# A cross-attention kernel: the Gram product of a group in 9 matmuls instead of 12, with its low diagonal handled through a column of the value product

## The reference, cut to what matters

```python
probs_t = softmax(q @ k_t.T * attn_scale)            # per head, 112 x 371
text_out = probs_t @ v_t
qsem = l2norm(probs_t @ text_ehs)                    # per head, 112 x 512
sem = qsem @ l2norm(ip_ehs).T                        # per head, 112 x 4
fused = q @ k_ip.T * attn_scale + 0.5 * sem
probs_ip = softmax(fused) * spatial_mask
out = (text_out + probs_ip @ v_ip) @ W_out + b_out + hidden_states
```

## Time and profile before

| | |
|---|---|
| median of 3 runs | 386.72 us (385.99 to 387.68) |
| profiled execution, first to last instruction (span) | 384.5 us |
| its own time | not on the page |
| mean granted TensorE clock | 0.998 |
| TensorE busy | 374.8 us, 97% |
| VectorE, ScalarE, GpSimd busy | 225.0, 213.2, 208.1 us |
| HBM traffic | 97 GB/s |

### The profile page before, as it was taken

One profiled execution on the slowest core, in us unless ns is written; L12 is line 12 of the kernel. 1 busy time (PEld: TensorE's weight loads), 2 busy tenths in 40 slices (PEclk: granted clock), 3 DMA queues, 4 the chain that ended last, 5 costly groups with the idle time before them and its releaser, 6 DMA issues.

```text
span 384.5 us, 9489 instructions
## 1 busy us (share of the span) xinstructions
PE 374.8 (97%) x3610; PEld 320.3 (83%) x3610; DVE 225.0 (59%) x498; ACT 213.2 (55%) x498; POOL 208.1 (54%) x229
## 2 busy tenths in 40 slices
PE   8999999998999999999999999999999999999996
PEld 6879898777888888888888888888888888888774
DVE  4998462774457536664556646664556656654454
ACT  6834145575556554646556554646555476458742
POOL 7020470675448652796248642796258443855972
PEclk9999999999999999999999999999999999999999
DMA  8999998276027420571227430581207310001000
GB/s 252 321 241 182 201 213 157 82 162 140 9 72 166 78 72 2 157 147 24 76 73 162 81 87 2 160 147 20 77 2 174 59 43 3 2 2 57 2 3 31
DMA packets 30001, 37.88 MB, mean 99 GB/s; under 512 B 14378, under 2 KB 27163, under 8 KB 29275
## 3 DMA queue, kind: packets, MB, share of 16 engines
q1 hardware_dynamic: 29588, 36.87, 41.3%
q10 hardware_dynamic: 368, 0.41, 0.4%
HBM read 28.36 MB, written 8.81 MB: 97 GB/s over the span
## 4 chain that ended last, share of the span: by engine, by line
PE 84%; DMA 6%; DVE 5%; ACT 2%; issue 1%; SPq 1%; DVEq 0%; ACTq 0%
PE PR L1078 39%; PE Y L1078 27%; PE O L1078 9%; PE P L1078 7%; DMA qst<-ma 3%; DVE mx L950 2%; DMA Vt<-wk 2%; PE PR L1269 1%; DMA qd<-kst 1%; PE PR L1206 1%; DVE kst L904 0%; DVE kst L902 0%; ACT big L796 0%; SPq L507 0%; SPq L427 0%
## 5 line engine op out<-in xcount | busy, mean ns | idle before, releaser
L620 POOL TENSOR_TENSOR pb<-pb 128x448 f32<-128x448 f32 x78 | 89.1, 1143 | 97.2 <-DVE pb L974 91.8
L950 DVE TENSOR_REDUCE mx<-PR 112x1 f32<-112x371 f32 x160 | 82.0, 537 | 75.2 <-PE PR L1078 74.9
L1078 PE MATMUL Y<-er,Gh 128*128 128x448 f32 x240 | 95.2, 397 | 0.7 <-ACT er L800 0.3
L974 DVE TENSOR_TENSOR pb<-big,Y 128x448 f32<-128x448 f32 x120 | 72.7, 620 | 33.6 <-PE Y L1078 33.4
L1078 PE MATMUL Y<-er,Gl 128*128 128x448 f32 x240 | 87.2, 363 | 0.0
L796 ACT ACTIVATE big<-P 128x448 f32<-128x448 f32 x120 | 65.2, 544 | 31.6 <-PE P L1078 31.4
L800 ACT ACTIVATE er<-big 128x448 fp32r<-128x448 f32 x120 | 69.3, 578 | 3.8
L1078 PEld LDWEIGHTS Y<-er,Gh 128*128 128x128 f32 x240 | 45.1, 188 | 11.9 <-DVE pb L974 7.8
L1078 PE MATMUL PR<-kst,qst 96*112 96x371 bf16 x160 | 50.6, 329 | 0.5 <-ACT Vt L788 0.2
L1078 PEld LDWEIGHTS Y<-er,Gl 128*128 128x128 f32 x240 | 45.2, 188 | 2.2
L1078 PE MATMUL P<-qst,kst 99*128 99x112 bf16 x480 | 43.0, 213 | 1.6 <-DMA qst<-ma 1.5
(11 more groups left out here) (201 smaller groups left out, 679.9 us busy)
## 6 DMA issues: line engine op xcount, KB each, us to landing
et<-ctxT SPq DMA_DIRECT2D x7, 752.0 KB, 4.4
kst<-kd SPq DMA_DIRECT2D x7, 720.0 KB, 7.7
kd<-ks SPq DMA_DIRECT2D x16, 288.0 KB, 2.9
qst<-qd SPq DMA_DIRECT2D x48, 70.0 KB, 2.4
kst<-kd SPq DMA_DIRECT2D x7, 480.0 KB, 9.7
kst<-kd SPq DMA_DIRECT2D x9, 240.0 KB, 9.2
qd<-kst SPq DMA_DIRECT2D x4, 336.0 KB, 7.7
vx<-xr SPq DMA_DIRECT2D x8, 140.0 KB, 2.7
```

The lines of the kernel that those rows point to most:

```text
L620: pool.tensor_tensor(total, total, (pz, pm)[j], ALU.add).then_inc(s_S, 1)
L950: dve.tensor_reduce(mx[b % 2][:, h:h + 1], bank[0:S, 0:T], AX.X, ALU.max).then_inc(s_free[seq[u] % NR], 1)
L974: dve.tensor_tensor((pz, pm, pa[g % 2])[j], eb[g % 3][:, 448 * j:448 * j + 448], Y[y % 2][:, 0:448], ALU.mult).then_inc(s_P, 1)
L1078: return pe.matmul(o, st, mv, start=start, stop=stop, **kw)
```

## The change

G is kept in three full row blocks (`Gh`, `Gl` of 3 x 384), no longer doubled off the diagonal. Its diagonal blocks are packed: the stored block is the strict upper triangle of the high part, plus half the diagonal, plus the strict lower triangle of the low part. Since e^T G e is twice the sum over the upper half, the diagonal block needs no low matmul: a Gram product for block j takes 2j + 1 matmuls, 5, 3 and 1. `usel` has 2.0 instead of 1.0. The triangle of the low part has no place for its diagonal. So `lh`, half the low diagonal, is subtracted from every entry of `Gl` for its row and for its column, which makes the diagonal zero: a new matmul L (ones times `dl`) spreads the column's share over all rows, and VectorE subtracts both. What is taken away is (sum of e) times (sum of 2 `lh` e). A 23rd column of `Vt`, twice `lh`, gives the second factor, and `norms` multiplies it by the denominator and adds it back.

Two units are new in each batch. D, on VectorE: low diagonal (`dl`), its reduction (`lh`), mask on the diagonal blocks of `Gh`. L: on TensorE one matmul into a ring bank, on ScalarE the 23rd column, on VectorE three subtractions, the mask on the low blocks and their sum into `Gh`; the first Gram product of the batch waits for that sum (`s_wd`). The norms have two more instructions on VectorE. The masks come from DRAM by one more DMA. The strings of the order are rewritten: g2, g1 and g0 stand apart with other units between them, E and pT change places, and the scores, K and v move.

```diff
 NP = NTOK + 1
-MV = 22
+MV = 23
...
 CW = (128, 128, 64)
-GOFF = (0, 384, 640)
...
 STACK = ((0, 3), (1, 2), (2, 1))
-FILLS = 27
+FILLS = 28
 QFILLS = 5
-FIRST, REST = 2, 6
+FIRST, REST = 3, 6
...
-ROUNDS = ("S0 K0 m g m K1 S1 m v S2 m G0 m",
-          "S0 m g m K2 C m S1 v m S2 G1 m",
-          "S0 m g2 T0 T1 g1 g0 m r0 S1 m pw v S2 m V0 m",
-          "Kr S0 r1 m g m V1 m S1 m m v r2 mT S2 z GV",
-          "p E g2 g1 pT g0 S0 cT S1 v o S2")
-SECOND = "K0 S0 m g m K1 S1 m v S2 m G0 m"
-NO_K = "S0 m m g m S1 v S2 m G0 m"
-EARLY = ("m S1- m S2- K1 S0 m g m S1 m S2 K2 m",
-         "S0 m g m S1 m S2 v m m wo C",
-         "S0 m g m S1 m S2 v m m",
-         "Kr S0 m m g m S1 m v mT S2 GV",
-         "E g S0 v S1 S2")
-LATE = "p g2 g1 pT g0 S0 cT S1 v S2 o"
-LAST = ("S0 v g2 S1 g1 S2 g0 T0 T1",
-        "S0 r0 g2 pw S1 g1 g0 pv S2 v",
-        "S0 r1 g2 S1 g1 r2 g0 S2 v",
+ROUNDS = ("K0 S0 m g2 m g1 S1 m K1 m S2 m g0 v G0",
+          "S0 m g2 g1 m S1 m g0 K2 C v m S2 G1 m",
+          "S0 m g2 T0 T1 g1 m g0 r0 S1 m pw S2 m v V0 m",
+          "Kr r1 m g2 g1 S0 m m g0 V1 S1 m m S2 v r2 mT z GV",
+          "p g2 pT E g1 D cT S0 S1 v g0 L o S2")
+SECOND = "S0 K0 m g2 g1 m S1 m g0 K1 m v S2 m G0"
+NO_K = "m m S0 g2 m g1 v g0 S1 S2 m m G0"
+EARLY = ("m S1- m S2- K1 S0 m g2 g1 S1 m m g0 m S2 K2",
+         "S0 m g2 g1 S1 m g0 S2 m v m m wo C",
+         "S0 m g2 g1 m S1 g0 m m S2 v m",
+         "Kr S0 m S1 m g2 m g1 m v g0 S2 mT GV",
+         "E g2 g1 S0 g0 D v S1 S2 L")
+LATE = "p g2 pT g1 S0 g0 D cT S1 L S2 v o"
+LAST = ("S0 S1 v g2 S2 g1 T0 T1 g0",
+        "S0 r0 g2 g1 pw v S1 g0 pv S2",
+        "S0 r1 g2 S1 r2 g1 g0 S2 v",
         "S0 g2 S1 z g1 p g0 S2 v",
-        "pT g2 T0' pw' r0' cT g1 g0 r1' v vW T1' r2' pv'")
+        "pT T0' pw' r0' g2 cT g1 g0 r1' v vW T1' r2' pv'")
...
     order += [("G", 0, 0)] + split(1)[:2] + [("G", 0, 1)] + split(1)[2:] + [("G", 0, 2)] + [("K", 1, c) for c in range(3)] + [("Kr", 1)]
-    side = [("V", 0, 1), ("V", 0, 2)] + [("qip", b) for b in range(B)]
+    order += [("D", 0)]
+    side = [("V", 0, 1), ("L", 0), ("V", 0, 2)] + [("qip", b) for b in range(B)]
...
         else:
+            if u[0] == "D":
+                out, held = out + held, []
...
 
-RING = ("K", "G", "V", "GV", "T", "pT", "cT", "o", "max", "mT")
+RING = ("K", "G", "V", "GV", "L", "T", "pT", "cT", "o", "max", "mT")
...
 
-def last_g(b):
-
-    return ("GV", b) if b else ("G", 0, 2)
+def g_pieces(b):
+
+    return [("G", b, 0), ("G", b, 1), ("GV", b) if b else ("G", 0, 2)]
...
         wol = sb("wol", [128, 3, C], f32r)
-        Gh = [sb(f"Gh{i}", [128, 768], f32r) for i in range(2)]
-        Gl = [sb(f"Gl{i}", [128, 768], f32r) for i in range(2)]
+        Gh = [sb(f"Gh{i}", [128, 3, TP], f32r) for i in range(2)]
+        Gl = [sb(f"Gl{i}", [128, 3, TP], f32r) for i in range(2)]
+        dl = sb("dl", [128, 3, 128], f32r)
+        lh = sb("lh", [128, 3])
+        ones_r = sb("ones_r", [128, 128], f32r)
+        tri = sb("tri", [128, 2, 128])
+        lq = sb("lq", [S, H])
...
                         act.wait_ge(s_gram, 3 * NG * (b - 1))
-                    a = min(128, T - 128 * i)
-                    act.activation(Gh[b % 2][0:r, GOFF[i]:GOFF[i] + a], bank[0:r, 0:a], ACT.Copy)
-                    rest = T - 128 * i - a
-                    if rest:
-                        act.activation(Gh[b % 2][0:r, GOFF[i] + a:GOFF[i] + a + rest], bank[0:r, a:a + rest],
-                                              ACT.Copy, scale=2.0)
+                    act.activation(Gh[b % 2][0:r, i, 0:T - 128 * i], bank[0:r, 0:T - 128 * i], ACT.Copy)
...
                                    ACT.Copy).then_inc(s_gh, 1)
+                elif k == "L":
+                    b = u[1]
+                    act.wait_ge(s_dl, 2 * b + 2)
+                    if b < 2:
+                        act.wait_ge(s_set, FILLS)
+                    else:
+                        act.wait_ge(s_pv, NG * (b - 1))
+                    act.activation(Vt[b % 2][:, :, :, 22], lh[:, :].unsqueeze(2).broadcast_to([128, 3, H]),
+                                   ACT.Copy, scale=2.0).then_inc(s_lc, 1)
...
                                   ALU.mult).then_inc(s_kb, 1)
+
+            def norms(hs, square):
+                if square:
+                    dve.tensor_tensor(t1[:, hs], R[:, hs, 20], R[:, hs, 20], ALU.mult)
+                link(dve.tensor_tensor(lq[:, hs], R[:, hs, 20], R[:, hs, 22], ALU.mult))
+                link(dve.tensor_tensor(lq[:, hs], lq[:, hs], R[:, hs, 21], ALU.add))
+                dve.scalar_tensor_tensor(ssq[:, hs], t1[:, hs], EPS * EPS, lq[:, hs], ALU.mult, ALU.max).then_inc(s_clamp, 1)
...
                     dve.wait_ge(s_gh, 3 * b + i + 1)
-                    gh, gl = Gh[b % 2], Gl[b % 2]
-                    a = min(128, T - 128 * i)
-                    rest = T - 128 * i - a
-                    o = GOFF[i]
-                    low = dve.tensor_tensor(gl[0:r, o:o + a], bank[0:r, 0:a], gh[0:r, o:o + a].bitcast(f32), ALU.subtract)
-                    if rest:
-                        low = dve.scalar_tensor_tensor(gl[0:r, o + a:o + a + rest], bank[0:r, a:a + rest], 2.0,
-                                                       gh[0:r, o + a:o + a + rest].bitcast(f32), ALU.mult, ALU.subtract)
-                    low.then_inc(s_free[seq[u] % NR], 1)
+                    gh, gl = [p[b % 2][0:r, i, 0:T - 128 * i] for p in (Gh, Gl)]
+                    dve.tensor_tensor(gl, bank[0:r, 0:T - 128 * i], gh.bitcast(f32),
+                                      ALU.subtract).then_inc(s_free[seq[u] % NR], 1)
...
                     dve.wait_ge(s_gh, 3 * b + 3)
-                    gh, gl = Gh[b % 2][0:r, GOFF[2]:GOFF[2] + a], Gl[b % 2][0:r, GOFF[2]:GOFF[2] + a]
+                    gh, gl = [p[b % 2][0:r, 2, 0:a] for p in (Gh, Gl)]
                     dve.tensor_tensor(gl, bank[0:r, C:C + a], gh.bitcast(f32), ALU.subtract).then_inc(s_free[seq[u] % NR], 1)
+                elif k == "D":
+                    b = u[1]
+                    if b == 0:
+                        dve.wait_ge(s_w, 16 * FIRST)
+                    else:
+                        filled(dve, ("L", b - 1))
+                        dve.wait_ge(s_lc, b)
+                    for piece in g_pieces(b):
+                        freed(dve, seq[piece])
+                    dve.scalar_tensor_tensor(dl[:, :, :], Gl[b % 2][:, :, 0:128].bitcast(f32), 0.5,
+                                             ident[:, :].unsqueeze(1).broadcast_to([128, 3, 128]),
+                                             ALU.mult, ALU.mult).then_inc(s_dl, 1)
+                    dve.wait_ge(s_dl, 2 * b + 1)
+                    dve.tensor_reduce(lh[:, :], dl[:, :, :].bitcast(f32), AX.X, ALU.add).then_inc(s_dl, 1)
+                    diag = Gh[b % 2][:, :, 0:128]
+                    dve.tensor_tensor(diag, diag.bitcast(f32), tri[:, 0, :].unsqueeze(1).broadcast_to([128, 3, 128]),
+                                      ALU.mult).then_inc(s_wu, 1)
+                elif k == "L":
+                    b = u[1]
+                    filled(dve, u)
+                    dve.wait_ge(s_dl, 2 * b + 2)
+                    for i in range(3):
+                        r, w = ROWS[i], T - 128 * i
+                        gl = Gl[b % 2][0:r, i, 0:w]
+                        low = dve.scalar_tensor_tensor(gl, gl.bitcast(f32), lh[0:r, i:i + 1], bank[0:r, 128 * i:T],
+                                                       ALU.subtract, ALU.subtract)
+                    low.then_inc(s_free[seq[u] % NR], 1)
+                    diag, low = Gh[b % 2][:, :, 0:128], Gl[b % 2][:, :, 0:128]
+                    freed(dve, seq[u])
+                    dve.tensor_tensor(low, low.bitcast(f32), tri[:, 1, :].unsqueeze(1).broadcast_to([128, 3, 128]),
+                                      ALU.mult).then_inc(s_wu, 1)
+                    dve.wait_ge(s_wu, 2 * b + 2)
+                    dve.tensor_tensor(diag, diag.bitcast(f32), low.bitcast(f32), ALU.add).then_inc(s_wd, 1)
...
                         ps = powers(b, 2)
-                        link(dve.tensor_tensor(t1[:, ps], R[:, ps, 20], R[:, ps, 20], ALU.mult))
-                        dve.scalar_tensor_tensor(ssq[:, ps], t1[:, ps], EPS * EPS, R[:, ps, 21], ALU.mult, ALU.max).then_inc(s_clamp, 1)
+                        norms(ps, True)
...
                     last.then_inc(s_ring, 1)
+                elif k == "L":
+                    b = u[1]
+                    if b == 0:
+                        pe.wait_ge(s_set, FILLS)
+                    pe.wait_ge(s_dl, 2 * b + 1)
+                    mm(bank[:, 0:TP], ones_r[:, :], dl[:, :, :].rearrange("p c n -> p (c n)"), True, True).then_inc(s_ring, 1)
...
                     if j == 2 and r == 0:
-                        freed(pe, seq[last_g(b)])
+                        pe.wait_ge(s_wd, b + 1)
...
                     d = Y[y % 2][:, 0:448]
-                    for i in range(j + 1):
```

(9 more changed lines are left out.)

35 lines of the change are left out of this document (22 added, 13 removed).

## The result

The changed kernel takes 390.24 us (median of 7, 388.17 to 392.15), the kernel before 386.72: a ratio of 1.0092, 95% interval 1.0072 to 1.0113. It is slower by 0.9%, which is beyond the interval; 378.6 was forecast. All ratios leave out executions more than 1.5% above the fastest of the same kernel, the medians do not. Its profiled execution has a span of 387.0 us.

The account below looks back on a forecast made before the run. TensorE, busy 97% of the span, was taken as the bound. Its own -22.8 us, plus 4.0, 3.0, 1.4, 3.6, 2.3 and 0.4 lost, gave -8.1: time 378.6, range 368 to 387.5.

Parts of the forecast that it names:

- El first: Round 5, batches 1 to 4: GpSimd's El starts before D, TensorE stands 2.2 us a batch; one of three equally weighted cases.
- the clock: TensorE's granted clock in the new stands: expected to stay at 1.00, no cost in the sum.
- TensorE's own account: All batches: matmuls dropped -24.0, product waits gone -5.7, L matmuls +2.9, extra crossings +4.0, together -22.8 us.
- D against El: Round 5, batches 1 to 4: D and El exclude each other, TensorE stands before o; 1.0 a batch, +4.0 us.
- rival (c): No change: El first in each batch (8.8 us) and pT 1.0 late (6.0), time 386.4; chance 0.16.
- VectorE's amount: Steady batch: VectorE's work grows about 4 us, from 24.2 to 28 of 40, no bound by amount.
- rival (d): TensorE's clock falls in the new stands; chance under 2%.
- pT late: Six batches: pT is asked for earlier than GpSimd's chain delivers, 0.5 us late each, +3.0 us.
- Ahead of batch 0: Longer first fill, mask table's DMA, and D and L among the maxima on VectorE: +0.8 us (0 to 3).
- S0 of batch 1: It waits for a DMA starting from mT, so what is saved between the two is given back: +0.8 us.
- Batches 5 and 6: Rounds without El: only GpSimd's sums delay D, 0.7 us each, +1.4 (0 to 1.6).
- The end: Last batch: GpSimd's chain keeps only some 0.7 us of the saving, +2.3; the norms' two instructions add +0.4.

Follow-up runs that it names:

- e3: Changed kernel with GpSimd's El (low part of the context) of batches 3 to 7 cut from 376 to 8 columns, work left out: 380.0 us.
- e13: Changed kernel with each El instruction of GpSimd cut into four pieces, no order moved, nothing left out: 379.93 us.
- e1: Changed kernel with D and L of batch 0 moved behind the transpose of the maxima, mT(0): 387.86 us.
- e9: Changed kernel with matmuls nobody reads put into TensorE's stands in front of cTl and the row waits: median 386.4 us, six executions far apart.
- e10: Changed kernel with VectorE's diagonal work cut to 8 of its columns and L's matmul to 24 columns, most of the correction left out: 379.89 us.
- e5: Changed kernel with D right behind g2 and the split E with El behind cT in round 5 of batches 1 to 4: 388.17 us.
- e2: Changed kernel with D behind cT and L behind o in round 5 of batches 1 to 4: 389.97 us.
- e11: As e1, with the output weights' split in round 0 instead of round 1 of batch 0: 387.47 us.
- e15: Changed kernel with only the first of batch 2's three key transfers issued ahead of batch 1's rows of the maxima, two behind: 387.16 us.
- e4: Changed kernel with the key load of batch 2 issued behind the rows of the maxima of batch 1: 391.4 us.
- e12: Changed kernel with e1, e11, e5 with K0 behind g2, and S0 behind g0, cT and v in batches 5 and 6: 391.05 us.
- e17: Changed kernel with e1, e13, e15 and e12's order of batches 5 and 6, nothing left out: 369.37 us.
- e16: Changed kernel with e1, e13, e14, e12's batches 5 and 6, and S2 ahead of g0 in the last batch: 380.24 us.
- e14: Changed kernel with the row transfers of the maxima of batches 1, 6 and 7 issued on ScalarE's queue, not SyncE's: 392.38 us.

## Why the prediction was wrong

Two steps failed most: the weight given to "El first", and the clock, which was put at nothing. The forecast's terms can be laid on the same stretches, and so can its error:

| stretch | its terms | forecast | measured | missed |
|---|---|---|---|---|
| start to mT(0) | 0.8 | +0.8 | +4.0 | 3.2 |
| mT(0) to mT(2) | -5.7, 0.8, 2.0 | -2.9 | -1.2 | 1.7 |
| mT(2) to mT(6) | -11.4, 4.0, pT 2.0 | -5.4 | -1.4 | 4.0 |
| mT(6) to mT(7) | -2.85, pT 0.5, 0.7 | -1.65 | 0.0 | 1.65 |
| mT(7) to the end | -2.85, 0.5, 0.7, 2.3, 0.4 | +1.05 | +1.0 | 0 |
| sum | | -8.1 | +2.5 | 10.6 |

**TensorE's own account (-22.8) was right.** A steady batch where nothing stands is 2.9 us shorter (e3, e13), and of the 7.8 us of Y waits 1.7 are left.

**D against El: 4.0 taken, 10.0 measured (-11.4 became -1.4), of it 6.9 without the clock.** This is the first of the two steps. The mechanism was forecast with its place, and the price of "El first" at 2.2 a batch; the stands are 1.95, 1.41, 2.06 and 1.44. What failed was to give this case a third of the weight. El came first in all four batches of the profiled execution, by some 0.1 us, and in e1, e9 and e10 as well: El follows ScalarE's split behind the copy of pT, `dl` follows VectorE's product of g1, whose matmuls stand right behind pT, so the distance between them does not change from batch to batch. With four times 2.2, the prediction's own 8.8 of rival (c), the term would have covered the 6.9. In these four batches e3 takes back 10.2 us and e13 9.3. VectorE's amount was put too low as well, at 28 us a batch: it is 30.8, with the time for which the held instructions stand counted as busy, and 28.9 in e3. That it is no bound by amount holds. One reading of the prediction is loose: the instruction of 0.25 us at 379.62 has 32 columns, the two that it is set against have 80. The rows of e5, e10 and e13 show the lock without it.

**The clock: 0 taken, rival (d) under 2%. This is the other step.** Two falls in the steady batches cost 3.1 us (43.5 for 41.95, twice). The one ahead of mT(0) costs 1.1 to 1.8 (57.34 for 55.5 to 56.2 in the traces without it), the one at S0 of batch 1 about 1.0 (mT(0) to mT(2) takes 74.0 us in e9, for 75.0). That is an estimate of 5 to 6 us, half of the 10.6 missed, and it is spread over three rows of the table. The argument set the new stands against idle time that is spread over 20 and 35 us, whereas a new stand is in one piece. That this is the difference is likely and not shown: stands of 1.83 (e2), 2.04 (e1) and 2.15 us were not followed by a fall, one of 1.37 was. The Trainium skill (TensorE: Matmul & The Clock Gate, Part 1) says that the clock is held low by default and activity releases it. The rows agree in part: with matmuls that nobody reads in the stands, the profiled execution of e9 keeps it at 1.00 in the steady batches, but three of its six executions have a mean of 0.969 to 0.982.

**pT late: 3.0 taken, 0 measured.** TensorE stood 0.7 us for pT once, in the last batch, as before. In the steady batch GpSimd's last product for it ended at 221.03 and pT ran at 221.43, behind g2. TensorE's way from T to pT became 2.0 us shorter (15.1 for 17.1), as forecast. But the chain to GpSimd's last product became 0.8 shorter too (14.7 for 15.5), which the prediction had ruled out: ScalarE made the exponentials of z at once (219.38) and not 0.9 us after GpSimd had it ready. The slack fell from 1.6 to 0.4.

**Ahead of batch 0: 0.8 taken (0 to 3), 4.0 measured.** e1 takes back 3.8 at mT(0). The prediction named D and L among the maxima and gave them no price of their own. The wait for the mask table, which it did not foresee, is the longest idle time there, and by e10 still only 0.4 of it counts; VectorE's 4.0 us of D(0) and L(0) in a stretch where the maxima set the pace, and the fall of the clock in it, are the rest. By the traces without a fall, the stretch would have missed by 1.4 to 2.1 and not by 3.2.

**S0 of batch 1: 0.8 taken, 4.6 measured.** That the gain is given back was right, the reason not. The rows do not follow mT but the key load issued ahead of them: S0 comes 12.7 us after that load's issue before, 13.4 in the changed kernel, 13.1 in e1, 13.2 in e11, and 8.3 in e15 with half of it ahead. In e4, with the rows issued first, S0 waits 0.2 us. D(0) had made the load 2.6 us late, and in the shorter stretch behind it the stand grew to 5.35. The 2.0 us for g2 behind L were hidden under that stand; when it goes, 1.0 of them show (e15).

**Batches 5 and 6.** D beside GpSimd's sums cost 0.24 a batch and not 0.7. But S0, put nearer to mT, stood 2.15 us for the rows of batch 6, which is in no term. e12's order and e17's take 1.6 of it back.

**The end** came out as summed, by other terms: g2 waits 1.4 us for er, since S2 stands at the end of a round. No run gained there (e16 moved the wait to VectorE's product, 1.5 us).

## What to carry to other kernels

Price a new VectorE instruction with two SBUF operands by the GpSimd instruction that it may meet, not by its own columns, and cut long GpSimd instructions where they can meet: order moves only sent the loss elsewhere (e2, e5, e12), shorter pieces removed most of it. When two chains are too near to call but hang on the same event, take the worse case for every batch and not a mean. Where TensorE sets the time, give a fall of the clock a price beside each new stand: in the steady batches it was 1.5 us, nearly as much as the stand, and the stand's length did not tell whether it came. Before a wait is called the cost of a stretch, shorten the work behind it as well (e10): the longest wait can be the cheap part. Ahead of a small urgent transfer count the bytes already issued, and put a large load behind it in part.

## What the runs showed of the hardware

- A VectorE instruction with both operands in SBUF is held until the GpSimd instruction under way is over, whatever its size: 24 columns 1.72 us, 384 columns 2.08, 0.89 beside pieces of 0.6 (e13), 0.56 with GpSimd idle (e5). The Trainium skill (SBUF — State Buffer, Who interferes with whom) states such a lock for the whole instruction, and these rows agree.
- Stands of 1.95 and 2.06 us were followed by 1.2 GHz for part of the next 4 to 8 us (0.62 in 228 to 232), and so was one of 1.37 (0.59 in 360 to 364); stands of 1.41 and 2.15 us in the same trace were not. A fall cost a steady batch 1.5 us. The executions of one kernel scatter with it: 388.2 us at a mean clock of 0.976 to 392.2 at 0.964 for the changed kernel, 381.8 at 0.994 to 393.8 at 0.969 for e9. e17 scatters by 1.8 us, at 0.993 to 1.00.
- Transfers of 1.44 MB issued 4.6 us ahead hold up three small ones behind them: S0, which needs these, comes 12.3 to 14.0 us after the large load's issue in 13 traces, 8.3 with half of it ahead (e15). Issued from ScalarE's queue, with the query load ahead as well, they were no sooner (15.4 us, e14).
